# Constant products ahead of TensorE's waits in the two gather passes of a graph network

## What is computed

```python
# layer 0: maximum over the edges of a node
msgs = z[dst] @ Wd + z[src] @ Ws + edge_weight[:, None] * ww + bm
agg  = segment_max(msgs, dst)
x1   = layernorm(z + relu(z @ W1a + agg @ W1b + b1) @ W2 + b2)
# layer 1: attention and gates over the edges of a node
h  = x1 @ node_fc_W + node_fc_b;  hs, hd = h[src], h[dst]
a  = sum(hs * hd, -1)
t  = relu(einsum(he, rel_att_W1) + rel_att_b1)      # he = edge features @ edge_fc_W + b
g  = sigmoid(einsum(t, rel_att_W2) + rel_att_b2)
alpha, beta = segment_softmax(a, dst), segment_softmax(g, dst)
h_att, h_rel = weighted segment sums of hs @ node_att_W and hs @ rel_att_W
out = layernorm(x1 + gate * h_out + (1 - gate) * x1)
```

## Time and profile before

| | |
|---|---|
| median of the runs | 2290.52 us |
| lowest and highest | 2287.78, 2296.37 us |
| profiled execution, first to last instruction (span) | 2723.8 us |
| own time of the profiled execution beyond the span | not recorded |
| mean granted TensorE clock | 0.806 |
| busy: PE, PEld, DVE, ACT, POOL | 68%, 42%, 49%, 41%, 60% |

### The profile page before, as it was taken

One profiled execution on the slowest core, in us unless ns is written; L12 is line 12 of the kernel. 1 busy time (PEld: TensorE's weight loads), 2 busy tenths in 40 slices (PEclk: granted clock), 3 DMA queues, 4 the chain that ended last, 5 costly groups with the idle time before them and its releaser, 6 DMA issues. The chain is left out here.

```text
span 2723.8 us, 43235 instructions
## 1 busy us (share of the span) xinstructions
PE 1843.7 (68%) x9891; PEld 1146.6 (42%) x9891; DVE 1328.7 (49%) x5220; ACT 1115.3 (41%) x3305; POOL 1639.6 (60%) x1705
## 2 busy tenths in 40 slices
PE   4577777677767777655666766676776776766665
PEld 3122222222222222114355655565665665655565
DVE  3454555554444444324535544544544545445459
ACT  1233333333333333333544444444444444444448
POOL 3666666666767777646455655555565655555525
PEclk7689888888889888876867777777777777777788
DMA  8433333333333333323311221221112221211113
GB/s 228 144 120 124 109 116 118 125 109 109 121 109 114 101 123 110 124 80 87 116 46 47 54 51 48 52 51 49 51 51 50 53 52 49 52 48 50 49 44 119
DMA packets 115983, 235.04 MB, mean 86 GB/s; under 512 B 32909, under 2 KB 68230, under 8 KB 106422
## 3 DMA queue, kind: packets, MB, share of 16 engines
q0 software_dynamic: 52832, 109.39, 16.3%
q1 hardware_dynamic: 56522, 97.21, 9.7%
q10 hardware_dynamic: 6540, 27.42, 2.9%
HBM read 166.01 MB, written 67.89 MB: 86 GB/s over the span
## 5 line engine op out<-in xcount | busy, mean ns | idle before, releaser
L463 POOL DMA_INDIRECT d_region<-d_h,d_region x784 | 747.8, 954 | 534.2 <-issue 221.1
L209 POOL DMA_INDIRECT acc<-d_src_product,b_region x784 | 779.4, 994 | 378.6 <-issue 225.5
L651 PE MATMUL banks<-acc,b_region 64*128 64x512 f32 x1176 | 351.8, 706 | 213.9 <-ACT acc L756 99.4
L859 DVE SCALAR_TENSOR_TENSOR acc<-b_region,acc 128x128 f32<-128x128 f32 x784 | 271.4, 346 | 433.6 <-DMA acc<-d_src_product,b_region 416.8
L1577 DVE TENSOR_TENSOR acc<-acc,banks 128x160 f32 x784 | 252.5, 322 | 318.6 <-remote 124.0
L1376 PE MATMUL banks<-d_region 128*128 128x128 f32 x1568 | 306.0, 357 | 4.1 <-issue 3.8
L1379 PE MATMUL banks<-d_region,pick 128*128 128x128 f32 x1568 | 294.1, 346 | 11.6 <-issue 11.2
L651 PEld LDWEIGHTS banks<-acc,b_region 64*128 64x128 f32 x1176 | 109.8, 211 | 429.7 <-issue 188.3
L1379 PEld LDWEIGHTS banks<-d_region,pick 128*128 128x128 f32 x1568 | 277.4, 262 | 13.6 <-issue 13.4
L1376 PEld LDWEIGHTS banks<-d_region 128*128 128x128 f32 x1568 | 271.2, 260 | 10.3 <-issue 5.3
L870 DVE SCALAR_TENSOR_TENSOR acc<-acc,b_region 128x128 f32<-128x128 f32 x784 | 270.1, 345 | 7.5 <-remote 5.2
(11 more groups left out here) (261 smaller groups left out, 2450.3 us busy)
## 6 DMA issues: line engine op xcount, KB each, us to landing
d_runs<-acc SPq DMA_DIRECT2D x48, 1024.0 KB
acc<-ea ACTq DMA_DIRECT2D x25, 1024.0 KB
acc<-d_src_product,b_region POOLq DMA_INDIRECT x784
d_region<-d_h,d_region POOLq DMA_INDIRECT x784
d_region<-d_rel SPq DMA_DIRECT2D x49, 256.0 KB
hT<-xT SPq DMA_DIRECT2D x7, 448.0 KB, 6.9
d_src_product<-acc SPq DMA_DIRECT2D x7, 448.0 KB, 3.7
acc<-xrow SPq DMA_DIRECT2D x1, 3136.0 KB
```

The source lines that it names most:

```text
L209: pool.indirect_dma_start(self.rows[:, s, j, :], None, d["B"], bass.IndirectOffsetOnAxis(self.idx[:, k:k + 1], 0)).then_inc(self.gathered[ ...
L463: pool.indirect_dma_start(rows[:, s, :], None, table, bass.IndirectOffsetOnAxis(idx[:, s:s + 1], 0)).then_inc(gathered[q], 16)
L651: last = nc.tensor.matmul(bank[4 + n % 2 * 2 + h][:, :], wf[h * DE:(h + 1) * DE, m * P:(m + 1) * P], ea[h * DE:(h + 1) * DE, u % (2 * UC), ...
L859: nc.vector.scalar_tensor_tensor(rows[:, s, j, :], wwb, wgt[:, k:k + 1], rows[:, s, j, :], ALU.mult, ALU.add).then_inc(ch, 1)
```

## The change

A helper issues `n` products of the identity, read as 2-byte numbers: 128x128 stationary, 256 columns moving. The result goes to a place in PSUM that a later product overwrites and that nobody reads. In the second pass each of the five parts first waits for its credit, then issues two such products into its own bank, then waits for its inputs: ten in each step. In the first pass four stand in `mlp(u)` ahead of the wait for the ReLU before the third pair, and four at the head of `dots(u)`, all into bank 0; they are left out for units 49 to 89, while bank 0 is in use, and before group 174 a new wait (`h2d`) makes sure that its last reader is done. 57 units have them. The lists of DVE, ACT, POOL and SP are the same before and after.

```diff
+def idle_products(nc, t, to, n):
+    halves = t["ident"].bitcast(BF16)
+    for _ in range(n):
+        nc.tensor.matmul(to, halves[:, 0:P], halves[:, 0:2 * P], start=True, stop=True)
...
+PARTS_END = PART_DVE + PART_STEP * (NC4 - 1) + 6
+IDLE_RUNS, IDLE_EDGES = 4, 2
...
+            def fill(u):
+                if 2 * u < SHIFT_AT - 2 or 2 * u > PARTS_END + 4:
+                    idle_products(nc, t, bank[0][:, 0:2 * P], IDLE_RUNS)
             def mlp(u):
                 for m in range(M):
                     n = M * u + m
+                    if m == 2:
+                        fill(u)
                     if n >= 2:
                         pe.wait_ge(ra, n - 1)
...
             def dots(u):
+                fill(u)
                 pe.wait_ge(ra, 3 * (u + 1))
...
             for g in range(PG):
+                if g == PARTS_END:
+                    pe.wait_ge(h2d, NC4)
...
+            def fill(to):
+                idle_products(nc, t, to[:, 0:2 * P], IDLE_EDGES)
             def turn_rows(it, q):
                 s = q % NG
+                pe.wait_ge(hc, it * NG + (q - 1 + 1 + CREDIT))
+                fill(TURNED)
                 pe.wait_ge(gat[s], it * 64 + 64 * lap(q))
-                pe.wait_ge(hc, it * NG + (q - 1 + 1 + CREDIT))
...
             def scores(it, q):
+                pe.wait_ge(mn, it * NG + (q - 1 + 1 + CREDIT))
+                fill(SCORES)
                 pe.wait_ge(hc, it * NG + (q + 1 + CREDIT))
                 pe.wait_ge(wn, it * NG + (q + 1 + CREDIT))
-                pe.wait_ge(mn, it * NG + (q - 1 + 1 + CREDIT))
...
             def spread(it, q):
+                pe.wait_ge(rf, it * NG + (q - 1 + 1 + CREDIT))
+                fill(BOUNDS)
                 pe.wait_ge(mn, it * NG + (q + 1 + CREDIT))
                 pe.wait_ge(sl, it * NG + (q + 1 + CREDIT))
-                pe.wait_ge(rf, it * NG + (q - 1 + 1 + CREDIT))
...
             def turn_weights(it, q):
+                pe.wait_ge(wt, it * NG + (q - 1 + 1 + CREDIT))
+                fill(WEIGHTS)
                 pe.wait_ge(ex, it * NG + (q + 1 + CREDIT))
-                pe.wait_ge(wt, it * NG + (q - 1 + 1 + CREDIT))
...
             def sums(it, q):
+                pe.wait_ge(ad, it * (NG * GJ) + (q - 2 + 1 + CREDIT) * GJ)
+                fill(bank[5 + q % 2 * 2])
                 pe.wait_ge(wt, it * NG + (q + 1 + CREDIT))
                 pe.wait_ge(bw, it * NG + (q + 1 + CREDIT))
-                pe.wait_ge(ad, it * (NG * GJ) + (q - 2 + 1 + CREDIT) * GJ)
```

## The result

The changed kernel takes 2302.43 us (median of 5 runs, 2296.94 to 2304.88), the kernel before 2287.78 us beside it (2284.81 to 2296.37). The ratio is 1.006 [1.004, 1.008]: 14.7 us slower, a little over the 0.5% that the prediction took as the least that can be told from no change. The forecast was 2240 us, 50 us faster.

A forecast was written before the change was run, and what follows sets the result against it. The prediction took POOL's gathers as the frame, with half-clock TensorE steps making POOL late in the second pass. 73 - 22 + 0 = 51 us off 2290.5 gave 2240 us, range 2120 to 2345 us.

The forecast's parts named there:

- The frame: Both gather blocks: at 1.25 us a gather, POOL waits 178 us too long in the first pass, 293 us in the second.
- the 51 us: Whole kernel: net gain, 73 us from slow steps less 22 us lost, first pass 0.
- 201 us: Second pass: bound on the gain, POOL's waits for TensorE (48.6 us) and for unnamed releasers (152.9 us).
- x = 0.46 slow steps: Second pass, TensorE: share of steps at half clock, 90 of 196, each 0.81 us above POOL's 5.0 us; 73 us gain.
- The price of a constant product: TensorE: 0.13 us fast and 0.25 us slow each; ten in a step 1.3 us fast, 2.5 us slow.
- The granted clock of the second pass rises from 0.77 to over 0.9: Second pass, TensorE: a sign of being right, with a group taking about 6.2 us instead of 6.47.
- the clock rises but the group stays at 6.47 us (POOL or DVE had the end): Second pass: a sign of being wrong, the group of four gathers getting no shorter despite the higher clock.
- Where the products stand: Second pass, `scores` and `spread`: pairs behind `mn` and `rf` delay the real product 0.26 us each; costed at nothing.
- First pass: 57 units with eight products: taken as 0, bounds 59 us lost to 103 us gained.
- Next late is the index copy: Second pass: after the change POOL's wait for DVE's index copy, 46.9 us, would be late next.
- POOL alone, or anything but the clock, sets the end: Rival, chance 0.20: gathers at 1.25 us hide the products; time 2255 to 2290 us, set at 2285.
- The products lie on the ring: Rival, chance 0.25: pairs behind `mn` and `rf` add 102 us to a DVE-TensorE chain; from 2302 up, centred on 2349 us.

The follow-up runs named there:

- E1: The kernel before, unchanged, recorded a second time: 2285.10 us, ratio 0.9997 to the kernel before.
- E2: Changed kernel with the ten products of a step in the second pass alone, none in the first: 2295.48 us, 1.0039 to the kernel before.
- E12: Second pass with two of four gathers of each group left out and the ten products: 2190.44 us, 0.9579 to the kernel before.
- E3: Changed kernel with the eight products of a unit in the first pass alone, none in the second: 2289.66 us, 1.0015 to the kernel before.
- E16: Changed kernel with twice the products at each place of the first pass, none in the second: 2290.69 us, 1.0013 to the kernel before.
- E4: Changed kernel with no constant product in either pass, only the new waits and their order: 2287.55 us, 1.0008 to the kernel before.
- E10: Kernel before with DVE's gate product of the second pass cut into three 128x128 pieces: 2291.38 us, 1.0012 to the kernel before.
- E7: Second pass gathers fetch 64 of 128 rows, no products, waits ordered as in the change: 2253.87 us, 0.9852 to the kernel before.
- E6: Second pass's ten products, none in the first, with DVE's `references` penalty instruction in another form: 2301.11 us, 1.0061 to the kernel before.
- E8: Second pass gathers fetch 64 of 128 rows, with the ten products there: 2255.96 us, 0.9856 to the kernel before.
- E9: Kernel before with DVE's gate product of the second pass issued twice in a row: 2317.50 us, 1.0123 to the kernel before.
- E14: Kernel before with gate product in three pieces, DVE's index copy moved behind `lowest`, and the second pass's products: 2294.26 us, 1.0031 to the kernel before.
- E15: Changed kernel with one product instead of two at each second-pass place, none in the first: 2289.29 us, 1.0007 to the kernel before.

## Why the prediction was wrong

**The frame was the step that failed.** "POOL waits 178 us too long in the first pass and 293 us in the second" held for one recorded execution that was 433 us longer than the runs. The prediction named the 433 us, had no row for them, and still carried that execution's microseconds over to the median. In the recording that has the runs' length, POOL's idle time in the gathers beyond 0.33 us is one pause of 8.1 us in the first pass and one of 0.4 us in the second. There was no lateness to win back, and the 51 us were shares of it. The sign stood in the earlier trace rows: the releasers without a name, three quarters of the prediction's 201 us, are in no other recording.

**The second pass, and x = 0.46 slow steps.** The groups take 995.2/196 = 5.08 us, not 6.47, and TensorE's clock was 0.88, not 0.77. Whatever share of the steps was slow, none of them reached the end, since POOL did not pause for one: in E1, for instance, TensorE still waits 1.77 us for the gathered rows at the end of a step of 5.05 us (1702.59 to 1707.64), and in the changed kernel 1.15 us in one of 5.40 us, with all ten products in it. The steps of over 8 us that were reckoned with do not occur: the longest from one `turn_rows` to the next is 7.31 us in E1 and 7.42 in the changed kernel.

**The price of a constant product was right.** A pair holds back the next real product by 0.32 us (1702.50 to 1702.82) and 0.24 us (1703.17 to 1703.41), where 0.26 was taken. The number of products was right too (2416 = 57 x 8 + 196 x 10).

**The clock rose, and nothing came back.** "The granted clock of the second pass rises from 0.77 to over 0.9" came true, 0.88 to 0.96 (E2: 1.00). The prediction's own sign of being wrong was "the clock rises but the group stays at 6.47 us (POOL or DVE had the end)": the clock rose and the group stayed, though at 5.08 and 5.12 us. The Trainium skill (TensorE: Matmul & The Clock Gate, The HAM clock gate) puts the ramp penalty, told there of the clock's rise at the start of work, at under 1% of a typical kernel's span; the runs agree, with 0% back, net of the products, even in E12, where POOL is out of the way. The prediction had weighed that rule against a clock of 0.77 in the longer recording, and let the latter decide.

**"Where the products stand" was costed at nothing, and here the loss came in.** The text had the place (the pairs behind `mn` and `rf` push the real product back by 0.26 us each) and the cover (DVE has a whole step). That cover held: with all ten products TensorE still waits for rows, 1.15 us in the step above. What the text had no price for is that the pairs move DVE's gate product against POOL's gathers: 113 held instead of 73, and +8.0 us of gathers in the second pass.

**First pass: 0 taken, at most some 3 us found** (E3 +3, E16 +2, E4 without products +1, at the edge of what the runs tell), inside the bounds, with no price per product. The gathers there are longer than 0.945 us too (981 ns in E1): 325 of them start inside the two steps of DVE for a gathered tile (L859 and L870, both inputs in SBUF) and carry 26.6 of the 28.3 us above 784 times 0.945.

**The new `h2d` wait and the order of the waits: nothing, as taken** (E4). **"Next late is the index copy"**: POOL does not wait for it in E1's rows, but did as soon as the gathers were shortened (E10).

**The rivals.** "POOL alone, or anything but the clock, sets the end" is what bounds the kernel (E7), and is why nothing came back. It gave 2255 to 2290 and was 12 us too low at its upper end, because it took POOL's pace as given. "The products lie on the ring" had the sign, and by luck its lower edge of 2302 us, but not the mechanism: in E1 and in the changed kernel POOL never waits beyond 0.3 us in the stretch shown, so no ring sets the pace. The measured time lies within the 2120 to 2345 us that the prediction gave, on the other side of no change.

What stays open: the 3 us behind the last gather (that tail is 111 to 128 us long among kernels with the same code there), the 1 to 3 us in the first pass, why the first recording was so long, and why the products bring more gathers into the hold in E2 and E6 but not in E8. That the gate product's position is what decides was read and counted in the timelines and supported by E9, E10, E14 and E15; but no run moved that instruction alone.

## What to carry to other kernels

Before reading waits from a recorded execution, hold its span against the runs' median; where they differ by more than the runs do, take another recording, since its waits need not be those of the runs. Waits without a named releaser on several engines were a second sign here. If the engine with the pace idles only for its fixed pause before each instruction, no earlier signal from the other engines can make the program faster; ask instead what they do to the length of its instructions. Filling an engine's pauses need not be free even where it has slack, because it shifts what hangs on its results against what runs by another rhythm.

## What the runs showed of the hardware

An indirect gather on POOL that starts 0.05 to 0.40 us into DVE's gate product (0.56 us, two inputs in SBUF) ends 0.81 us after the product: it lasts up to 1.33 us in E1, against 0.945 us alone. Issuing the product twice in each of 196 groups added 26 us to the gathers, and cutting it in three took 11.6 of 16.2 us of the hold away. Of the 200 gathers of E1 that start inside `add_windows`, which has one input in PSUM, none is held. In the first pass, where L859 and L870 follow each other without a pause from 73.61 to 77.89 us of E1, a gather that starts among them is held through the whole run:

```profile
74.30 4.48 POOL L209 DMA_INDIRECT acc<-d_src_product,b_region  x1 [0.30 <-issue]
```

The Trainium skill (SBUF — State Buffer, SBUF: two separate sides) describes the port pair that DVE and GpSimd share as an exclusive lock, held for the whole instruction, and counts a DVE instruction with two SBUF inputs among its holders against a GpSimd instruction that reads SBUF; the held gathers agree with it, with their constant 0.81 us behind the product's end. The same page of the Trainium skill (Who interferes with whom) tells of a probe in which a `tensor_tensor` did not hold up a DMA; here, where the gather takes its row numbers from SBUF, it did.

A gather of 64 rows lasts 0.925 us on average (E7), one of 128 rows 0.966 (E1): halving the rows takes 4% off. And TensorE's clock went from 0.88 to 1.00 in the second pass at a time 0.4% longer (E2).
